# Routing of a sparse expert layer beside the node update of a graph layer: batches, engines and a second pass

## What is computed

```python
xn   = layernorm(x)
gate = sigmoid(silu(edge_attr @ W1 + b1) @ W2 + b2)            # per edge
aggr = segment_sum(gate * xn[src], dst)
upd  = silu(concat([xn, aggr]) @ U1 + c1) @ U2 + c2
x    = x + xn + upd + mix(xn)                                   # mix: linear attention, folded into a 256x256 matrix
xn2  = layernorm(x)                                             # the "second norm"
logits = xn2 @ gate_w + gate_b                                  # 16 experts
two best experts per node, weights by softmax over the two
x    = x + sum over the two of weight * ((silu(xn2 @ w1[e]) * (xn2 @ w2[e])) @ w3[e])
```

## Time and profile before

| | us |
|---|---|
| median of three runs | 1153.02 |
| the profiled execution | 1151.01 |
| its span, first to last instruction | 1149.2 |
| TensorE busy | 1050.9 (91%) |
| VectorE busy | 896.5 (78%) |
| GpSimd busy | 761.7 (66%) |
| ScalarE busy | 670.3 (58%) |

### The profile page before, as it was taken

The page is one execution under the profiler, slowest core; times in us unless marked ns, Lnnn a source line. Parts: engine busy times, 40 slices in busy tenths (PEclk is TensorE's granted clock), DMA queues, the critical chain, the costliest instruction groups (busy, mean ns, idle before and its releaser), DMA issues.

```text
span 1149.2 us, 23535 instructions
## 1 busy us (share of the span) xinstructions
PE 1050.9 (91%) x7924; PEld 990.9 (86%) x7924; DVE 896.5 (78%) x1331; ACT 670.3 (58%) x1023; POOL 761.7 (66%) x720
## 2 busy tenths in 40 slices
PE   4897999999999999999999989983499999999992
PEld 2466899999999999999999889972499999999992
DVE  7877998888898888889988815858667777777770
ACT  2562766666666666666667434430067767677761
POOL 5457777777777777777777746401456777767752
PEclk9998999999999999999999979975899999999996
DMA  8211444454544444544444301222168888889864
GB/s 240 71 52 51 142 143 140 141 143 143 145 142 141 140 141 142 145 144 141 142 140 142 84 3 60 92 88 80 67 180 235 238 229 232 226 227 237 235 137 131
DMA packets 115689, 165.14 MB, mean 144 GB/s; under 512 B 15394, under 2 KB 88151, under 8 KB 115543
## 3 DMA queue, kind: packets, MB, share of 16 engines
q1 hardware_dynamic: 83942, 95.11, 26.0%
q0 software_dynamic: 31104, 68.19, 24.5%
q10 hardware_dynamic: 560, 0.79, 0.2%
HBM read 145.55 MB, written 21.68 MB: 146 GB/s over the span
## 4 chain that ended last, share of the span: by engine, by line
PE 85%; DVE 8%; issue 3%; ACT 1%; DMA 1%; PEld 1%; POOL 0%; DVEq 0%; POOLq 0%; ACTq 0%; PEldq 0%; SPq 0%
PE ps L1426 24%; PE ps L1595 16%; PE ps L1437 15%; PE ps L1607 8%; PE ps L1380 8%; PE ps L1482 3%; PE ps L1354 2%; PE ps L1499 2%; PE ps L1490 2%; PE ps L1582 1%; PE ps L1513 1%; PE ps L1363 1%; PE ps L1347 1%; PE ps L1364 1%; DVE st L917 1%
## 5 line engine op out<-in xcount | busy, mean ns | idle before, releaser
L1426 PE MATMUL ps<-fr 128*128 128x256 f32 x2352 | 306.9, 287 | 3.2 <-DVE fr L979 3.2
L1426 PEld LDWEIGHTS ps<-fr 128*128 128x128 f32 x2352 | 289.4, 192 | 4.1 <-DVE fr L979 4.1
L565 POOL DMA_INDIRECT big<-xn_rows,srcs x200 | 218.7, 1094 | 60.8 <-issue 60.8
L565 POOL DMA_INDIRECT hgx<-xn_rows,srcs x192 | 210.6, 1097 | 58.5 <-issue 58.5
L718 ACT ACTIVATE h1f<-ps,b 128x512 f32<-128x512 f32 x196 | 124.0, 684 | 165.6 <-PE ps L1380 164.4
L1437 PEld LDWEIGHTS ps<-oh,big 128*128 128x128 f32 x1568 | 192.9, 194 | 10.8 <-issue 2.8
L1595 PE MATMUL ps<-fr 128*128 128x256 f32 x1536 | 192.5, 285 | 2.7 <-issue 1.4
L1437 PE MATMUL ps<-oh,big 128*128 128x96 f32 x1568 | 191.2, 276 | 2.6 <-DVE big L1115 2.6
L1595 PEld LDWEIGHTS ps<-fr 128*128 128x128 f32 x1536 | 189.0, 194 | 3.3 <-issue 1.8
L979 DVE TENSOR_TENSOR fr<-h1f,fr 128x1024 fp32r<-128x1024 f32 x98 | 120.1, 1225 | 52.7 <-ACT fr L721 52.6
L1292 DVE TENSOR_TENSOR fr<-big,fr 128x1024 fp32r<-128x1024 f32 x96 | 117.4, 1223 | 30.3 <-ACT fr L831 29.9
(11 more groups left out here) (190 smaller groups left out, 1387.6 us busy)
## 6 DMA issues: line engine op xcount, KB each, us to landing
big<-in_w SPq DMA_DIRECT2D x128, 256.0 KB, 4.2
rbf<-in_rbf SPq DMA_DIRECT2D x98, 256.0 KB, 2.9
big<-in_w SPq DMA_DIRECT2D x32, 512.0 KB, 4.0
xn_rows<-xn SPq DMA_DIRECT2D x38, 128.0 KB, 1.7
big<-xn_rows,srcs POOLq DMA_INDIRECT x200, 3.1
out<-out_rows SPq DMA_DIRECT2D x1, 3125.0 KB, 11.7
hgx<-xn_rows,srcs POOLq DMA_INDIRECT x192, 3.2
out_rows<-x_nodes SPq DMA_DIRECT2D x3, 768.0 KB, 3.7
```

What stands on the lines that cost most here:

```text
L565: pool.indirect_dma_start(hg[i % HB][:, s, :], None, xn_d[:, :], bass.IndirectOffsetOnAxis(srcs[:, col:col + 1], 0))\
L1426: last = mm(ps[:, 2 + 4 * p + s // 2, (s % 2) * D:(s % 2 + 1) * D], h1s[p][a][:, c, s * P:(s + 1) * P], W2s[b][:, c, :], start=c == 0 and ...
```

## The change

- **Second norm.** xn2 moves from VectorE (`tensor_scalar`) to ScalarE (`activation` with Identity, scale rstd and bias -mean * rstd; VectorE makes that bias, `nmr`, with one more linked instruction per chunk). Four buffers instead of two, and four for the transposes. Chunks are now (0,6), (6,12), (12,16), (16,20), (20,25). `XN2AT` says after which pair ScalarE makes which tiles; tiles 0 to 19 go beside the pairs, 20 to 24 after them, through the banks 6, 7, 0, 1. SyncE stores tile by tile in that order.
- **Routing in three batches** of 6, 6 and 13 tiles (`RCUT`). A batch is counted by `count`: VectorE adds the two one-hots, takes the running sum over its tiles, carried on from the batch before, and TensorE makes two matmuls whose sum in PSUM is the rank of each choice within its expert (`upto` is `before` minus one; `ones` times the running sum). `ranks` picks a choice's rank and splits it in low and high. Batch 0 and 1 are found and counted beside the pairs (VectorE in pairs 7, 9, 10; TensorE's `count(0)` behind `node_silu(9)`; the second half of `node_xn(11)` also waits for `s_rk`, since `ranks(0)` reads the same bank). `low_marks(0)` is made in pair 11.
- **Slot table.** Since expert blocks begin at multiples of 256, low needs only the rank; high needs the expert's offset (`places`). In four chunks of 6, 6, 6 and 7 tiles VectorE alone makes the marks; the first pass places only token numbers (50 matmuls of 80 columns).
- **Weights in a second pass.** After `tab`, VectorE turns each high mark into the weight (`weight_marks`, behind `w_low(0, 0, 0)` and ahead of `slots_low(0, 0)`), and 50 more matmuls of 80 columns sum them in bank 6: 24 ahead of the first transposes (`turn`), 26 between these and the first `expert_up`. `dest` and `wslot` follow, with a second step of `s_tabi` that `copy_y` and `scatter_slots` wait for. GpSimd no longer has `weigh`, and the first four gathers take their indices straight from `tab`.
- TensorE's first steps of `s_uo` and `s_ux` stand at the kernel's beginning, and its wait for `s_gnn` is gone, so ScalarE may make the high part of the first normed rows earlier.

```diff
 SB = 256
-CH = 6
-CHUNKS = [(t, t + CH if t + 2 * CH <= NT else NT) for t in range(0, NT - CH, CH)]
+CHUNKS = ((0, 6), (6, 12), (12, 16), (16, 20), (20, NT))
 NB = -(-NT // 2)
-LAG = 8
-TC = 5
+XN2AT = {3: (0, 2), 4: (2, 4), 5: (4, 6), 6: (6, 8), 7: (8, 10), 8: (10, 12), 9: (12, 14), 10: (14, 18), 11: (18, 20)}
+RCUT = (0, 6, 12, NT)
+XN2B = 4
+TCUT = (0, 6, 12, 18, NT)
+NTC = len(TCUT) - 1
+TAILB = (6, 7, 0, 1)
+RBANK = (4, 3, 4)
 XCUT = (0, 2, 4, 10, 16, NT - 1)
 KLAG = 9
 KVCUT = (0, 6, 12, 18, 22, NT)
...
+            def store_xn2(t):
+                sp.wait_ge(s_xn2, t + 1)
+                sp.dma_start(xn2_d[t * P:(t + 1) * P, :], xn[t % XN2B]).then_inc(s_xn2st[t % XN2B], 16)
+            for v in range(NB):
+                for t in range(*XN2AT.get(v, (0, 0))):
+                    store_xn2(t)
+                for t0, end in CHUNKS:
+                    if (end - 1) // 2 == v:
+                        sp.wait_ge(s_x1, v + 3)
+                        sp.dma_start(acc_d[t0 * P:end * P, :].rearrange("(t p) d -> p t d", p=P), x[:, t0:end, :])\
+                            .then_inc(s_acc, 16)
...
             for t in range(*CHUNKS[-1]):
-                sp.wait_ge(s_xn2, t + 1)
-                sp.dma_start(xn2_d[t * P:(t + 1) * P, :], xn[t % 2]).then_inc(s_xn2st[t % 2], 16)
+                store_xn2(t)
...
             def gather_slots(i, p):
                 pool.wait_ge(s_xsp, i + 1)
-                pool.tensor_copy(idx[p][:, 0:2], tab[:, ds(i * 2, 2)]).then_inc(s_sidx, 1)
-                pool.wait_ge(s_tabi, 1)
-                pool.wait_ge(s_sidx, i + 1)
+                if type(i) is int and i < 4:
+                    at = tab[:, 2 * i:2 * i + 2]
+                    pool.sem_inc(s_sidx, 1)
+                else:
+                    at = idx[p][:, 0:2]
+                    pool.tensor_copy(at, tab[:, ds(i * 2, 2)]).then_inc(s_sidx, 1)
+                    pool.wait_ge(s_tabi, 1)
+                    pool.wait_ge(s_sidx, i + 1)
                 for s in range(2):
                     pool.indirect_dma_start(xs[p][:, s, :], None, xn2_d[:, :],
-                                            bass.IndirectOffsetOnAxis(idx[p][:, s:s + 1], 0))\
-                        .then_inc(s_xs[p], 16)
+                                            bass.IndirectOffsetOnAxis(at[:, s:s + 1], 0)).then_inc(s_xs[p], 16)
...
+            def xn2(t):
+                act.wait_ge(s_rs, next(k for k in range(len(CHUNKS)) if CHUNKS[k][1] > t) + 1)
+                if t >= XN2B:
+                    act.wait_ge(s_xn2st[t % XN2B], t // XN2B * 16)
+                    act.wait_ge(s_tp2, t - XN2B + 3)
+                act.activation(xn[t % XN2B], x[:, t, :], ACT.Identity, scale=rstd[:, t:t + 1], bias=nmr[:, t:t + 1])                    .then_inc(s_xn2, 1)
...
+            for v in range(NB):
+                if v + 1 < NB:
+                    u1_silu(v + 1, (v + 1) % 2, min(2, NT - 2 * v - 2))
+                tiles = range(*XN2AT.get(v - 1, (0, 0)))
+                late = range(*XN2AT.get(v - 2, (0, 0)))[2:]
+                for t in late:
+                    copy_lg(t, 6 + t % 2)
+                for t in tiles[:2]:
+                    copy_xt2(t, t % 2, 6 + t % 2)
+                if v + 3 < NB:
+                    node_high(v + 3, (v + 3) % 2, min(2, NT - 2 * v - 6))
+                for t in tiles[:2]:
+                    copy_lg(t, 6 + t % 2)
+                for t in tiles[2:]:
+                    copy_xt2(t, t % 2, 6 + t % 2)
+                for t in range(*XN2AT.get(v, (0, 0))):
+                    xn2(t)
+
+            for t in range(NT - 5, NT - 1):
+                xn2(t)
+            for i in range(4):
+                copy_xt2(NT - 5 + i, i, TAILB[i])
+                if i == 0:
+                    xn2(NT - 1)
+            copy_lg(NT - 5, TAILB[0])
+            copy_lg(NT - 4, TAILB[1])
+            copy_xt2(NT - 1, 0, TAILB[0])
+            copy_lg(NT - 3, TAILB[2])
+            copy_lg(NT - 2, TAILB[3])
+            copy_lg(NT - 1, TAILB[0])
...
             block_steps(0, 0, 0, 0)
+            act.wait_ge(s_tabi, 2)
...
+            for v in range(NB):
+                n = min(2, NT - 2 * v)
+                x1(v, v % 2, n)
+                dve.wait_ge(s_x1, v + 3)
+                for k in range(n):
+                    last = stats(2 * v + k)
                 link(last)
...
+                for t0, end in CHUNKS:
+                    if (end - 1) // 2 == v:
+                        for t in range(t0, end):
+                            last = moments(t)
+                        link(last)
+                        layer_stats(t0, end - t0)
+                        link(dve.scalar_tensor_tensor(nmr[:, t0:end], mv[:, t0:end, 0], -1.0, rstd[:, t0:end],
+                                                      ALU.mult, ALU.mult))
+                        dve.sem_inc(s_rs, 1)
+                if v == 7:
+                    top2(0, 6)
+                    count(0)
+                if v == 9:
+                    ranks(0)
+                if v == 10:
+                    top2(6, 12)
+                    count(1)
+                if v == 11:
+                    low_marks(0)
+            top2(12, 20)
+            ranks(1)
+            low_marks(1)
+            top2(20, NT)
+            count(2)
             link(dve.tensor_tensor(exw[:, :], top[:, 1, :], top[:, 0, :], ALU.subtract))
             dve.sem_inc(s_dif, 1)
-            for k in range(2):
-                link(dve.tensor_scalar(ohx[k][:, NT - 1, :], ohx[k][:, NT - 1, :], valid[:, 0:1], None, ALU.mult))
-            link(dve.tensor_tensor(m12, ohx[0], ohx[1], ALU.add))
-            dve.sem_inc(s_m12, 1)
...
+            dve.wait_ge(s_cnt, 2)
+            link(dve.tensor_scalar(c_i[:, :], ps[:, RBANK[2], D + 13 * NX:D + 14 * NX], float(SB - 1), None, ALU.add))
             link(dve.tensor_scalar(c_i[:, :], c_i[:, :], SB.bit_length() - 1, None, ALU.arith_shift_right))
             link(dve.tensor_copy(c_e, c_i[:, :]))
-            link(dve.tensor_tensor_scan(cend, onerow[:, 0:NX], c_e, 0.0, ALU.mult, ALU.add))
+            link(dve.tensor_tensor_scan(cend, ones[:, 0:NX], c_e, 0.0, ALU.mult, ALU.add))
             link(dve.tensor_tensor(off, cend, c_e, ALU.subtract))
-            link(dve.scalar_tensor_tensor(off, off, float(SB), t_ex[:, :, 0], ALU.mult, ALU.subtract))
-            link(dve.tensor_tensor(t_a, t_ex.rearrange("p e t -> p t e"),
...
+            def places(a, b):
+
+                n = 2 * (b - a)
+                each = lambda ap: ap[:, a:b, :, :].rearrange("p t k e -> p (t k) e")
+                link(dve.tensor_tensor(each(t_b), each(ohk), off.unsqueeze(1).to_broadcast([P, n, NX]), ALU.mult))
+                link(dve.tensor_reduce(hsel[:, a:b, :], t_b[:, a:b, :, :], X, ALU.add))
+                link(dve.scalar_tensor_tensor(hif[:, a:b, :], hsel[:, a:b, :], float(SB // P), shi[:, a:b, :],
+                                              ALU.mult, ALU.add))
+
...
+            def high_marks(c):
+
+                shape = [P, 2 * (TCUT[c + 1] - TCUT[c]), NS]
+                link(dve.tensor_tensor(tB[c], iota[:, 0:NS].unsqueeze(1).to_broadcast(shape), over(hif, c, shape),
+                                       ALU.is_equal))
+                dve.tensor_tensor(tB[c], tB[c], over(tok, c, shape), ALU.mult).then_inc(s_hot, 1)
+
+
+            def weight_marks(c):
+
+                shape = [P, 2 * (TCUT[c + 1] - TCUT[c]), NS]
+                dve.wait_ge(s_tab, c + 1)
+                dve.scalar_tensor_tensor(tB[c], tB[c], 0.5, over(wts, c, shape), ALU.is_ge, ALU.mult).then_inc(s_hot, 1)
+            places(0, 12)
+            high_marks(0)
+            high_marks(1)
+            ranks(2)
+            low_marks(2)
+            places(12, NT)
+            high_marks(2)
...
-            dve.wait_ge(s_tab, 2 * NT // TC + 2)
+            low_marks(3)
+            high_marks(3)
+            dve.wait_ge(s_ex, 1)
+            link(dve.tensor_scalar(v_a[:, 0:NT], exw[:, :], 1.0, None, ALU.add))
+            link(dve.reciprocal(wts[:, :, 0], v_a[:, 0:NT]))
+            link(dve.tensor_tensor(wts[:, :, 1], wts[:, :, 0], exw[:, :], ALU.mult))
+            link(dve.tensor_scalar(wts[:, NT - 1, :], wts[:, NT - 1, :], valid[:, 0:1], None, ALU.mult))
+
+            dve.wait_ge(s_tab, NTC)
             held, row = tf
-            link(dve.tensor_copy(wslot[:, :], ps[:, 2, NS:2 * NS]))
             link(dve.tensor_scalar(held, ps[:, 2, 0:NS], 1.0, None, ALU.is_ge))
             link(dve.tensor_tensor(row, ps[:, 2, 0:NS], held, ALU.subtract))
             link(dve.tensor_copy(tab[:, :], row))
-            link(dve.tensor_tensor(row, row, spare[:, :], ALU.subtract))
-            link(dve.tensor_tensor(row, row, held, ALU.mult))
-            link(dve.tensor_tensor(dest[:, :], row, spare[:, :], ALU.add))
             dve.sem_inc(s_tabi, 1)
 
 
@@ -1320,8 +1388,16 @@
                 if not last:
                     w_low(1, i + 1, 1 - p)
             w_low(0, 0, 0)
```

(79 more changed lines are left out.)

283 lines of the change are left out of this document (101 added, 182 removed).

## The result

| | before | after |
|---|---|---|
| median of 9 runs each, one beside the other | 1151.21 us | 1158.22 us |
| span of the profiled execution | 1149.2 us | 1157.1 us |
| start of the node pairs | 671.79 | 671.02 |
| last `x1` starts | 759.04 | 765.65 |
| `tab` (before: `dest`) done | 824.15 | 812.86 |

A forecast was written before the change was run, and what follows sets the result against it. VectorE working alone through routing and marks was taken as the bound. Last `x1` at 763.7 plus 67.8 put the first `expert_up`'s end at 831.5, 6.7 us earlier, giving a median of 1146.3 us, range 1138.5 to 1155.

The forecast's parts named there:

- the clock of the second pass: From `place` to first `expert_up`: starts at 1.2 GHz, rises after 13 matmuls; 24 matmuls 8.1 us, 26 5.7, `expert_up` 2.9.
- the rival: The slower rival, chance 0.12.
- The same assumption, in the first pass: First pass, before `tab`: the last 14 placing matmuls run at 1.2 GHz after 4.6 us of waiting, 6.1 us.
- The gather: Behind `tab`: starts at 48.4 us from the last `x1`, rows at 53.2, covered by the second pass.
- Beside the pairs: Node pairs: VectorE's added work and meetings with GpSimd stall TensorE 1.5 and 1.8 us; last `x1` 4.7 us later, at 763.7.
- The start: Start of the node pairs: first rows done earlier, 0.55 us less, bounds 0 and 1.2.
- ScalarE: Beside the pairs: stays free with 4.6 of 7.07 us per pair used, xn2 taken at 0.45 us.
- the rival in which Identity needs a table of its own: Node pairs: two 1.28 us loads per pair bring ScalarE to 7.2 of 7.07 us; 1150 us, chance 0.04.
- Behind the pairs up to `tab`: Last `x1` to `tab`: scales 4.05 us, last logits 12.1, `high_marks(0)` 24.0, `high_marks(3)` 41.1, `tab` 48.0.
- The rule on shared ports: Gather beside `weight_marks`: its issue could wait for all of them until 54.2, rows at 59.0, sum 0.3 us longer.
- The slower rival: Second pass: TensorE stays at 1.2 GHz, 78.8 us from last `x1` to first `expert_up`'s end; 1157.3 us, chance 0.12.

The follow-up runs named there:

- e1: Changed kernel with the placing matmuls of both passes streaming their 80 columns twice (160): 1152.22 us, ratio 0.9991 to the kernel before.
- e7: Changed kernel with only the second pass's placing matmuls streaming their 80 columns twice (160): ratio 0.9988 to the kernel before.
- e6: Changed kernel with the semaphore steps that let GpSimd gather moved ahead of the placing matmuls: ratio 1.0152 to the kernel before.
- e2: Changed kernel with the second pass left out, so without the slots' weights, only to price that pass: 1139.25 us, ratio 0.9887 to the kernel before.
- e3: Changed kernel with the first batch's `top2` and `count` moved to pair 6 and `ranks(0)` directly behind `x1(9)`: 1152.3 us, ratio 0.9995 to the kernel before.
- e4: Changed kernel with one pass of 50 matmuls of 160 columns, token and weight marks side by side: 1144.69 us, ratio 0.9928 to the kernel before.
- e5: Changed kernel with the edits of e3 and e4 together: ratio 0.9934 to the kernel before.

## Why the prediction was wrong, point by point

**The step that failed: the clock of the second pass.** "I let it start low too: 13 matmuls at 0.434, 11 at 0.22", then "26 matmuls 5.7" and an `expert_up` of 2.9. I took the 5.6 us after which the clock had risen behind a first `expert_up` of 256 columns and carried it to matmuls of 80. The nearest rows spoke against it: the earlier trace rows had 96 columns, seven microseconds of them, and the clock rose only as they ended, and I had put them under the rival. Term by term, forecast and measured: first 24 matmuls 8.1 and 10.53; `turn` 0.5 and 1.09; 26 matmuls 5.7 and 11.01; `expert_up` 2.9 and 4.96. Together 10.4 us of the 12.7 by which the first `expert_up` missed 831.5; the pairs add 2.0 and the gather 1.1, and the way to `place(4)` was 0.7 shorter. e1 and e7 show that it is the clock and not the number of matmuls: with twice the columns the same passes take less time.

**The same assumption, in the first pass,** was made the other way (the last 14 matmuls low, 6.1 us) and held: 6.25.

**The gather: a missed step.** I let it start at 48.4 and called it covered. It hung on an increment in TensorE's program behind `place(5)`, which the diff moves by putting six `place` ahead of it. It cost 1.07 us; e6 shows it. I had gone through what the change moves on GpSimd's queue and not on TensorE's.

**Beside the pairs: right mechanism, sizes 2.0 short.** `x1(8)` was forecast 11.6 us behind `x1(7)` and came 12.1 behind; the stalls were forecast 1.5 and 1.8 us and were 2.11 and 1.51. That a stall of 2 us can cost the clock as well, and 1.5 us more, was not in the sum. The last `x1` came at 765.65 instead of 763.7. In e1 and e2 it came at 762.7 and 763.1, by the same 1.5 and by the 1.1 us in the first 24 entries. e3 removes both stalls. The kernel before has 5.49 us in these first 24 entries as well, so they are no part of the loss.

**The start**: forecast -0.55, measured -0.77. **ScalarE** stays free, although xn2 cost 0.59 a tile where I took 0.45. **Tables**: the rival in which Identity needs a table of its own falls. ScalarE's groups from 640 to 860 us hold two table loads, for exp and for the experts' silu, and none between silu and Identity in the pairs:

```profile
L839 ACT ACT_TABLE_LOAD x1 | 1.3, 1283 | 0.0
L857 ACT ACT_TABLE_LOAD x1 | 1.3, 1283 | 0.0
```

This agrees with the Trainium skill, ScalarE: Activation LUTs, section "Table sets: the hidden batching unit", which has identity in every set.

**Behind the pairs up to `tab`: right within 1.1 us.** From the last `x1`: scales 4.0 (4.05), last logits 11.5 (12.1), `high_marks(0)` 23.5 (24.0), `high_marks(3)` to 40.0 (41.1), `tab` 47.2 (48.0). The marks cost 1.16 for 960 elements and 1.33 for 1120, where the line through two prices gave 1.14 and 1.30. From `tab` to `place(4)` 2.7 us (2.6).

**The rule on shared ports.** I weighed the Trainium skill, SBUF — State Buffer, section "Who interferes with whom", as 0.3 us, if a gather's issue waited for all four `weight_marks`. In e6 three issues took 0.4, 0.9 and 1.1 us more than 0.95, so each was held up by no more than about one mark, and the first was through before the second mark began. That agrees with a lock held for one instruction, as that section has it. VectorE's marks (1.15) were not stretched. That the first gather would wait for all four marks did not come. Their rows were still there before `place(5)` had ended.

**From there to the end.** Of the 7.9 us between the two spans 6.0 are there at the first `expert_up`. Another 1.3 come at the end: the last `expert_down` took 4.44 us instead of 3.12, because the clock fell in the 2.29 us before it. The same pause stands in all 13 profiled kernels; the matmuls behind it took 4.3 to 4.6 us in nine of them and 3.1 in four (the kernel before, e2, e4, e5). The change doesn't touch that place, and what decides it is not shown. The forecast had no term for it.

**The chances.** The slower rival had its price right (78.8 us from the last `x1`; 78.6 measured), with parts that cancel: the wait for the gather was missing, the way to `place(4)` and the first `expert_up` were taken too long. It had a chance of 0.12. A forecast that hung on one assumption about the clock, with the nearest row against it, should have given that rival far more, a third at least by my judgement, and the range its whole width.
